# Split stores by terms, an earlier start of the first attention, and a causal mask by select, in a two-block transformer

## The chip, the cores and the metric

The kernel runs on one core of a Trainium2 chip. The metric is the device time of one execution in microseconds. In the text PE is TensorE, ACT ScalarE, DVE VectorE, POOL GpSimd and SP the sync engine, which here only issues DMAs.

## What is computed

`x` has one batch of 1024 rows of 128, the context `ctx_1024` has 6404 rows of 128. Four attentions of 16 heads of 8 follow each other, with mixtures of experts and a feed-forward layer between them (cut to what matters; layer norms, experts and residuals are left out):

```
cross0: softmax(where(mask, -inf, (x Wq) (ctx Wk)^T / sqrt(8))) (ctx Wv) Wproj     # 1024 x 6404, key padding mask
self0:  softmax((x Wq) (x Wk)^T / sqrt(8)) (x Wv) Wo                               # 1024 x 1024
self1:  the same with a causal mask: key t counts for query s only where t <= s
cross1: softmax((x Wq2) (ctx Wk2)^T / sqrt(8)) (ctx Wv2 + bv2)                     # 1024 x 6404, no mask
```

## The kernel before, in words

The order of the work is: setup of cross0, cross0, setup of self0, self0, experts, setup of self1, self1, setup of cross1, cross1, feed-forward, experts. Each engine has its own program (`block.sync`, `block.gpsimd`, `block.scalar`, `block.vector`, `block.tensor`), and these meet only at semaphores.

**Setup of an attention.** Queries and keys are projected in fp32 in jobs of 512 columns (`projection_plan`, `project`), and each job's result is split into three bf16 parts: ACT copies part 1 from PSUM (L937), DVE subtracts it for the rest (`take_rest`, L1104 is the helper `tt` that records all such subtractions), ACT copies part 2 (L942), GpSimd subtracts for part 3 (L753). For cross0 DVE first multiplies the keys with the mask (`keep`, L1176, `whole`) and makes a row of -BIG for the masked keys (L1162). SP stores the parts in DRAM (`store_parts`, L511 keys, L515 queries), four buffers in a ring (`SPLITS`). Keys are stored as three parts, queries as six terms (`Q_PARTS`), a head's 48 rows together. Cross0 has 13 key jobs and 2 query jobs; before them the context is transposed by PE (L1846) and evacuated by ACT (L917), and before that the layer norm of `x` is made and transposed by PE (`turn`). After the keys SP loads the mask row and a row of ones into every slot (`load_mask_row`, L498, L501), then stores the queries, then waits for all stores (`all_stored`).

**Staging.** A pass (one head and half of the queries in a cross attention; two heads and half of the queries in a short one) needs rows in SBUF: 48 rows of keys for each of two sides (6404 keys are cut in two halves, or there are two heads) and 48 rows of queries, in a ring of four slots. Keys come by three DMAs a side, for 3, 2 and 1 parts (`stage_keys` L529, `stage` L600), queries by one a side for each of two copies (L540, L543, L602). SP issues them in the order written: four passes ahead at first, then one a pass.

**A pass.** Pass A computes scores to find each query's maximum (`pass_a`, 28 units a pass in a cross attention, DVE reduces each, L1234 and L1193; `join_maxima`). GpSimd splits the maxima in three parts (`split_maxima`, L783, L811), PE turns them (`turn_maxima`, L1578, L1709), ACT copies them (L966, L1009), and SP puts them as three more rows behind the queries (`put_maxima`, L612, L551). Pass B computes the scores with keys on partitions less the maximum (`pass_b`), ACT makes exps into `probs` (`exps`, L1028, L986) out of a ring of three PSUM banks, and PE multiplies with the values (`values`), three steps later in a short attention, five in a cross attention. All matmuls are recorded on the helper line L1498. Maxima run ahead of pass B: 40 units before the first pass B of a cross attention, among which the 13 banks of values are projected.

**Early keys.** Cross1's keys depend on the context alone. In cross0's passes 18 to 30 one of 13 key blocks is put among the maxima (`a.items`): PE projects it, DVE copies it out (L1244), GpSimd makes all three parts (L845 to L848) and SP stores it.

**Causal mask.** In self1 pass A and pass B add -BIG where a key is ahead of the query, by a matmul of `ident_b` with `causal_a` or `causal_b` into the scores' bank, for diagonal tiles only. GpSimd's loop in a short attention is: `split_maxima(j + 1)`, then in even passes `stage_pair`, which copies values.

Of the kernel before, what the change touches and what calls it, by code (L numbers as in the profile page):

```python
# [26 lines left out]
U8 = mybir.dt.uint8  # L27
# [36 lines left out]
def projection_plan(a):  # L64

    k_jobs = [("k", "masked" if a.masked else "plain", c, min(BANK, a.keys - c)) for c in range(0, a.keys, BANK)]
    q_jobs = [("q", "plain", c * BANK, BANK) for c in range(HALVES)]
# [12 lines left out]
def short_plan(name, keys, causal):  # L80
# [7 lines left out]
    a.stage_dmas = 4 * a.sides  # L88
# [33 lines left out]
def cross_plan(name, keys, masked, early_jobs):  # L122
# [23 lines left out]
    a.stage_dmas = 4 * a.sides  # L146
# [25 lines left out]

    a.early_from, n = 16, len(a.max_units)
    early = {(a.early_from + 2 + i) * n + 4: i for i in range(early_jobs)}
    a.items, a.items_with = [], [0]
    for v in range(a.n * n):
        if v in early:
            a.items.append(("key", early[v]))
        a.items.append(("max", v))
        a.items_with.append(len(a.items))  # L180
    a.key_item = {i: k for k, (kind, i) in enumerate(a.items) if kind == "key"}
# [4 lines left out]
def transformer(nc, io, out):  # L186
    cross0 = cross_plan("cross0", 6404, masked=True, early_jobs=13)
# [10 lines left out]
    with ExitStack() as ctx:  # L198
# [17 lines left out]


# [18 lines left out]
        ROWS_IN = cross0.sides * cross0.ring * 3  # L236
# [21 lines left out]
        keep = probs_b[:, 0:S // 2].bitcast(BF16)  # L258
        mask_in = probs_b[:, S // 2:S // 2 + S // 4].bitcast(U8)
        drop_row = k_stages[0:1, 0:S]  # L260
        part_words = SPLITS * 3 * BANK // 2
        for a in attentions:


            if a.masked:
                a.whole, a.rest = scratch[:, 0:SPLITS * BANK], scratch[:, SPLITS * BANK:2 * SPLITS * BANK]
                a.parts = probs_b[:, 16 * BANK - part_words:16 * BANK]
            else:
                a.whole, a.rest = probs_b[:, 0:SPLITS * BANK], probs_b[:, SPLITS * BANK:2 * SPLITS * BANK]
                a.parts = probs_b[:, 2 * SPLITS * BANK:2 * SPLITS * BANK + part_words]  # L270
            a.whole = a.whole.rearrange("p (b n) -> p b n", b=SPLITS)
# [3 lines left out]


        early_whole, early_rest = (z[:, b * 4:(b + 1) * 4].rearrange("p t d -> p (t d)") for b in range(2))
        early_parts = xn[:].rearrange("p t d -> p (t d)")[:, 0:3 * BANK // 2].bitcast(BF16).rearrange(
            "p (t n) -> p t n", t=3)
# [51 lines left out]
        n_first = len(loads)  # L331
        weight("o_cross0", [P, D], io["L0_xattn_Wproj"])
# [1660 lines left out]
```

## Time and profile before

| | us |
|---|---|
| median of 3 runs | 2730.98 (2729.42 to 2733.01) |
| the profiled execution | 2728.58 |
| its span | 2726.7 |
| PE busy | 2384.8 (87%) |
| DVE busy | 2352.2 (86%) |
| ACT busy | 2134.0 (78%) |
| POOL busy | 274.8 (10%) |
| setup and first maxima of cross0, to the first pass B | 0 to 136 |
| cross0, passes | 136 to 1114 |
| self0, with its setup | 1114 to 1340 |
| self1, with its setup | 1394 to 1588 |
| cross1, setup | 1588 to 1631 |
| cross1 | 1631 to 2640 |

The busy shares are means over stages with different limits. In each stage the question is which wait ends last. The mean granted TensorE clock is 0.941 of full speed.

### The profile page before, as it was taken

Reading aid. Unit: us, or ns where it says so; the run is one execution under the profiler, and the core shown is the slowest. Engines: PE = TensorE matmul, PEld = TensorE weight load, DVE = VectorE, ACT = ScalarE, POOL = GpSimd, SP = SyncE. Lnnn points to the kernel's source line nnn. Section 1 sums busy time; section 2 is a strip of 40 time slices with the busy share of each in tenths; the row PEclk is TensorE's granted clock in tenths of the full one; section 3 lists DMA queues with packets and bytes.
Section 4 is the critical chain, followed back from the end, with each engine's and each line's share of the span. In section 5 each row is a group of like instructions: output and inputs, shape, how many; then the busy total and the mean of one; then the engine's idle time right before and its main releaser. Section 6 shows DMA issues by size and latency. Waiting matters only on the chain.

```text
span 2726.7 us, 59202 instructions
## 1 busy us (share of the span) xinstructions
PE 2384.8 (87%) x23163; PEld 751.8 (28%) x23163; DVE 2352.2 (86%) x2668; ACT 2134.0 (78%) x4065; POOL 274.8 (10%) x740
## 2 busy tenths in 40 slices
PE   4499999999999999489758848999999999999986
PEld 2222222222222222122322213222222222222224
DVE  6699999999999997499636649999999999999945
ACT  3189999999889899469615625999999999999971
POOL 5000110012111110100001100000000100000000
PEclk8799999999999999789878968999999999999998
DMA  4201111111111110111121030111111111111000
GB/s 144 73 24 41 41 35 45 43 44 41 47 49 41 41 43 7 46 50 33 36 61 41 30 99 4 38 34 30 30 40 33 30 30 41 31 30 32 17 3 8
DMA packets 75513, 107.98 MB, mean 40 GB/s; under 512 B 17061, under 2 KB 55849, under 8 KB 75241
## 3 DMA queue, kind: packets, MB, share of 16 engines
q1 hardware_dynamic: 73128, 99.79, 12.4%
q0 software_dynamic: 2112, 4.42, 0.9%
q8 instruction: 189, 3.10, 0.5%
q14 instruction: 84, 0.68, 0.1%
HBM read 73.45 MB, written 21.90 MB: 35 GB/s over the span
## 4 chain that ended last, share of the span: by engine, by line
PE 68%; DVE 18%; ACT 5%; SPq 3%; issue 3%; DMA 2%; POOL 0%; ACTq 0%; DVEq 0%
PE ps L1498 68%; DVE maxima L1234 12%; ACT probs L1028 4%; SPq L515 1%; DVE maxima L1193 1%; SPq L600 1%; ACT probs L986 1%; DVE scratch L1104 1%; DMA o_self<-acc_out 0%; PE ps L1504 0%; DVE stats L1110 0%; DMA scratch<-o_self 0%; DMA q_stages<-max_rows 0%; DVE z L1104 0%; DMA q_stages<-q_cross 0%
## 5 line engine op out<-in xcount | busy, mean ns | idle before, releaser
L1234 DVE TENSOR_REDUCE maxima<-ps 128x1 f32<-128x920 f32 x1792 | 1887.8, 1111 | 96.4 <-PE ps L1498 96.3
L1028 ACT ACTIVATE probs<-ps 128x512 f32<-128x512 f32 (+1 forms) x3264 | 1761.3, 594 | 159.9 <-PE ps L1498 159.7
L1498 PE MATMUL ps<-probs,v_stage 128*16 128x256 f32 x14208 | 1159.5, 393 | 0.6 <-ACT acc_out L1017 0.4
L1498 PE MATMUL ps<-k_stages,q_stages 64*128 64x460 bf16 (+2 forms) x4032 | 756.3, 373 | 187.3 <-DMA q_stages<-q_cross 64.4
L1498 PE MATMUL ps<-q_stages,k_stages 64*128 64x512 bf16 (+1 forms) x3712 | 725.8, 381 | 45.1 <-ACT probs L986 16.9
L1498 PEld LDWEIGHTS ps<-k_stages,q_stages 64*128 64x128 bf16 x4032 | 193.6, 93 | 1049.7 <-issue 494.3
L1498 PEld LDWEIGHTS ps<-probs,v_stage 128*16 128x16 f32 x14208 | 236.9, 94 | 412.2 <-issue 362.9
L1193 DVE TENSOR_REDUCE maxima<-ps 128x2 f32<-128x1024 f32 (+1 forms) x224 | 240.1, 1108 | 94.5 <-PE ps L1498 90.9
L986 ACT ACTIVATE probs<-ps 128x512 f32<-128x512 f32 x448 | 224.2, 554 | 72.7 <-PE ps L1498 71.7
L1498 PEld LDWEIGHTS ps<-q_stages,k_stages 64*128 64x128 bf16 x3712 | 187.4, 93 | 277.4 <-ACT probs L1028 69.4
L952 ACT ACTIVATE by_key<-ps 128x512 f32<-128x512 f32 (+1 forms) x30 | 17.5, 583 | 146.2 <-PE ps L1498 146.2
L759 POOL COPY v_stage<-by_key 128x400 f32<-128x400 f32 x64 | 33.1, 517 | 901.1 <-PE ps L1498 785.8
L811 POOL CAST half_parts<-neg_max 128x4 bf16<-128x4 f32 x64 | 11.9, 187 | 851.4 <-DVE neg_max L1253 794.5
L1104 DVE TENSOR_TENSOR scratch<-scratch 112x512 f32<-112x512 f32 (+1 forms) x14 | 13.6, 982 | 66.0 <-DMA scratch<-acc_out 39.7
L904 ACT ACTIVATE std<-var_eps 128x4 f32<-128x4 f32 x18 | 3.7, 205 | 70.9 <-DVE var_eps L1116 70.9
L1104 DVE TENSOR_TENSOR probs<-ps,probs 128x512 f32<-128x512 f32 x36 | 24.5, 689 | 19.8 <-ACT probs L1088 8.2
L1017 ACT ACTIVATE acc_out<-ps 128x512 f32<-128x512 f32 x64 | 38.2, 597 | 0.3 <-PE ps L1498 0.3
L1504 PE MATMUL ps<-ident,z 128*128 128x128 f32 x32 | 8.1, 403 | 32.0 <-DVE z L1126 18.5
L1504 PE MATMUL ps<-ident,xn 128*128 128x128 f32 x24 | 6.6, 430 | 31.5 <-DVE xn L1104 18.0
L783 POOL CAST max_parts<-neg_max 128x8 bf16<-128x8 f32 x32 | 6.1, 189 | 208.5 <-DVE neg_max L1204 162.4
L753 POOL TENSOR_TENSOR probs<-probs 128x512 bf16<-128x512 f32 x10 | 11.2, 1151 | 149.8 <-ACT probs L942 149.8
L1104 DVE TENSOR_TENSOR z<-ps,z 128x512 f32<-128x512 f32 (+2 forms) x10 | 6.7, 674 | 21.0 <-PE ps L1498 14.6
(233 smaller groups left out, 965.4 us busy)
## 6 DMA issues: line engine op xcount, KB each, us to landing
q_stages<-q_cross SPq DMA_DIRECT2D x256, 48.0 KB, 2.6
k_stages<-k_cross SPq DMA_DIRECT2D x64, 150.2 KB
k_stages<-k_cross SPq DMA_DIRECT2D x64, 150.0 KB
scratch<-acc_out SPq DMA_DIRECT2D x496, 16.0 KB
k_stages<-k_cross SPq DMA_DIRECT2D x64, 100.1 KB
k_stages<-k_cross SPq DMA_DIRECT2D x64, 100.0 KB
q_stages<-q_self SPq DMA_DIRECT2D x32, 192.0 KB
k_cross<-probs SPq DMA_DIRECT2D x12, 384.0 KB, 2.8
```

The costliest lines, as they stand in the source:

```text
L515: sp.dma_start(a.q_dram[:, term * E:(term + 1) * E, c0:c0 + n], src[:, part, 0:n]).then_inc(done, DMA)
L600: sp.dma_start(k_stage(a, slot)[base + row:base + row + parts_ * E, :], a.k_dram[0:parts_, h * E:(h + 1) * E, :]).then_inc(done, DMA)
L759: nc.gpsimd.tensor_copy(v_stage[:, par, 0:full, 0:E], src[:, 0:full, :]).then_inc(sem(a.name + "_v_staged"), 1)
L952: last = nc.scalar.activation(by_key[:, t:t + full, :], src[:, 0:full, :], ACT.Copy)
L986: return nc.scalar.activation(probs[:, i % a.p_slots, low:BANK], ps[:, b_bank(a, use), low:BANK], ACT.Exp, scale=float(E) ** -0.5)
L1017: nc.scalar.activation(acc_out[:], ps[:, ACC_BANK, :], ACT.Copy).then_inc(sem(a.name + "_acc_copied"), 1)
L1028: return nc.scalar.activation(probs[0:m, probs_slot(a, j, i), :], ps[0:m, b_bank(a, use), :], ACT.Exp, scale=float(E) ** -0.5)
L1104: return nc.vector.tensor_tensor(out_, a, b, op)
L1193: nc.vector.tensor_reduce(pair_maxima[:, j % 2, :, qt % QT, c // BANK], ps[:, A_BANK + 2 * (g % 2):A_BANK + 2 * (g % 2) + 2, 0:n], AX_X, A ...
L1234: nc.vector.tensor_reduce(maxima[:, at, seg:seg + 1], ps[:, A_BANK + 2 * (k % 2):A_BANK + 2 * (k % 2) + 2, 0:a.segment], AX_XY, ALU.max).t ...
L1498: return nc.tensor.matmul(out_, lhsT, rhs, start=start, stop=stop)
L1504: last = nc.tensor.transpose(ps[:, bank, t * P:(t + 1) * P], src[:, b * QT + t, :], ident[:])
```

## The change

What it does, part by part. (1) The context is transposed first and the layer norm's result later, between the split jobs (`SETUP_TURNS`). `x` is loaded behind the first piece of context. The mask is loaded in one partition only, the keys are no longer multiplied with it, and the row of -BIG alone masks them. Constants that are needed later are made later on GpSimd. The mask row and ones row are loaded by 2 + 2 DMAs. (2) Key parts are stored as six terms, like the queries, in arrays `[TERMS, P, n]`, by three DMAs a job (`store_job`); ACT issues those of the last query job, and the stores waited for are fewer. Staging takes one DMA a side for keys. In a short attention the first pair takes half of its queries first (`stage_rest` for the others). (3) The 13 early key blocks move from cross0's passes to its first maxima (`a.fill`), with ACT making the copy and parts 1 and 2, GpSimd the rest and part 3. (4) In self1's even passes SP puts the maxima before it stages. (5) Pass B's causal mask matmuls are gone; GpSimd's `affine_select` writes zeros into the exps instead (`clear`), and `values` waits for it.

```diff
+        a.fill = [("values", i, n * (i + 1) // banks - (n * (i + 1) % banks == 0)) for i in range(banks)]
+        a.fill += [("key", i, 2 * i + 1) for i in range(early_jobs)]
...
+        def store_job(queue, a, i):
+            kind, c0, n = a.jobs[i]
+            src, done = a.parts[:, i % SPLITS, :, 0:n], stored(a, i)
+            queue.wait_ge(sem("split_part3"), a.jobs_before + i + 1)
+            first = 0
+            for part, terms in enumerate((3, 2, 1)):
+                if kind == "k":
+                    dst, part_ = a.k_dram, src[:, 0:terms]
+                else:
+                    dst, part_ = a.q_dram, src[:, part:part + 1].to_broadcast([P, terms, n])
+                queue.dma_start(dst[first:first + terms, :, c0:c0 + n].rearrange("a p c -> p a c"),
+                                part_).then_inc(done, DMA)
+                first += terms
...
             def stage_keys(a, j):
-                    for row, parts_ in ((0, 3), (3 * E, 2), (5 * E, 1)):
-                        sp.dma_start(dst[base + row:base + row + parts_ * E, 0:count],
-                                     a.k_dram[0:parts_, h * E:(h + 1) * E, first:first + count]).then_inc(done, DMA)
+                    sp.dma_start(dst[base:base + ROW_MAX, 0:count],
+                                 a.k_dram[:, h * E:(h + 1) * E, first:first + count]).then_inc(done, DMA)
...
+                if a is cross0:
+                    for i in range(len(early.jobs)):
+                        if i == len(early.jobs) - 2:
+                            put_maxima(0)
+                        store_job(sp, early, i)
+                else:
+                    put_maxima(0)
...
+                    if a.turn_step[j] == 0 and j + 1 < a.n:
+                        put_maxima(j + 1)
                     if half == 0 and pair >= 1 and pair + a.ring - 1 < H // 2:
                         ...
                         stage(pair + a.ring - 1)
-                    if j + 1 < a.n:
+                    if a.turn_step[j] != 0 and j + 1 < a.n:
                         put_maxima(j + 1)
...
+                def clear(j, t):
+                    if not is_diagonal(a, j, t):
+                        return
+                    kt, low = a.steps[j][t]
+                    width = (kt % QT + 1) * P - low
+                    for side in range(a.sides):
+                        i = pair_tile(a, j, t, side)
+                        pool.wait_ge(sem(a.name + "_probs"), i + 1)
+                        tile = probs[:, i % a.p_slots, low:low + width]
+                        nc.gpsimd.affine_select(out=tile, in_=tile, compare_op=ALU.is_ge, fill=0.0, base=P - width,
+                                                pattern=[[1, width]], channel_multiplier=-1).then_inc(sem("cleared"), 1)
                 for j in range(a.n):
                     pair, half = a.passes[j]
                     if j + 1 < a.n:
                         split_maxima(j + 1)
-                    if half == 0 and 1 <= pair < H // 2 - 1:
-                        pool.wait_ge(sem(a.name + "_batches"), a.batches_before[j])
-                        stage_pair(pair + 1)
+                    for t in range(len(a.steps[j])):
+                        if t == 2 and half == 0 and 1 <= pair < H // 2 - 1:
+                            pool.wait_ge(sem(a.name + "_batches"), a.batches_before[j])
+                            stage_pair(pair + 1)
+                        clear(j, t)
...
+            def take_early(i):
+                _, _, n = early.jobs[i]
+                b = i % SPLITS
+                act.wait_ge(sem("split_psum"), early.jobs_before + i + 1)
+                if i >= SPLITS:
+                    act.wait_ge(sem("split_rest"), early.jobs_before + i - SPLITS + 1)
+                    act.wait_ge(stored(early, i - SPLITS), stored_count(early, i - SPLITS))
+                whole = early.whole[:, b, 0:n]
+                nc.scalar.activation(whole, ps[:, EARLY_BANK, 0:n], ACT.Copy).then_inc(sem("early_whole"), 1)
+                act.wait_ge(sem("early_whole"), i + 1)
+                nc.scalar.activation(early.parts[:, b, 0, 0:n], whole, ACT.Copy).then_inc(sem("split_part1"), 1)
...
         pass_b:
-                    if diag:
-                        hi = (kt % QT + 1) * P
-                        for side in range(a.sides):
-                            bank = b_bank(a, pair_tile_use(a, j, t, side))
-                            mm(ps[:, bank, low:hi], ident_b[:], causal_b[:, 2 * P - (hi - low):2 * P],
-                               start=False).then_inc(sem(a.name + "_scores"), 1)
         values:
+                    if a.causal:
+                        pe.wait_ge(sem("cleared"), diagonals_before(a, j, 2 * b + 2))
...
+            def cross0_before(i):
+                if i in SETUP_TURNS:
+                    b = SETUP_TURNS.index(i)
+                    if b == 1:
+                        half_turned(0, 1)
+                    turn(b, xn, 1, 3)
```

## Rows read from the trace of the kernel before

**Rows 1.** Chain that ended last, setup: start us, us, what

```profile
55.87 0.87 SPq L498
...
71.57 0.59 SPq L515
...
81.21 0.78 SPq L529
...
85.50 7.81 DMA q_stages<-q_cross
...
100.55 24.64 DVE maxima L1234 x24
```

**Rows 2.** Timeline, setup of cross0: start us, us, engine line op

```profile
13.37 1.13 DVE L1126 TENSOR_SCALAR xn<-x,mean_var,rstd 128x128 f32<-128x128 f32 x4
...
22.70 1.02 PE L1498 MATMUL ps<-ctxT,w_kv_cross 128*128 128x512 f32 x2
...
40.03 0.63 ACT L937 ACTIVATE probs<-scratch 128x512 bf16<-128x512 f32 x1
...
42.11 1.22 POOL L753 TENSOR_TENSOR probs<-scratch,probs 128x512 bf16<-128x512 f32 x1 [1.29 <-ACT probs L942]
...
54.34 0.69 DVE L1104 TENSOR_TENSOR scratch<-ps,probs 128x512 f32<-128x512 f32 x1 [0.64 <-ACT probs L937]
```

**Rows 3.** Key stores: the page (last: us to landing) and SP issue ns

```profile
k_cross<-probs SPq DMA_DIRECT2D x12, 384.0 KB, 2.8
...
L511 SPq DMA_DIRECT2D k_cross<-probs x13: 359/360/392, 29.3 to 55.4; - x13
```

**Rows 4.** Windows: engines busy; at the end PEclk, DMA share, GB/s

```profile
95.00:100.00 5.00, 4.77 (x22) 3.41 (x22) 3.87 (x5) 0.60 (x1) 0.00 (x0) 0.54 0.36 118
...
1590.00:1595.00 5.00, 1.43 (x12) 1.32 (x12) 4.69 (x18) 0.85 (x2) 0.00 (x0) 0.96 0.25 88
```

**Rows 5.** Timeline, first maxima of either cross attention

```profile
135.93 0.64 PE L1498 MATMUL ps<-q_stages,k_stages 64*128 64x512 bf16 x2
...
1638.91 1.17 PE L1498 MATMUL ps<-w_v_cross,ctxT 128*128 128x128 f32 x8
```

**Rows 6.** Timeline, GpSimd, one row a pass: plain, then with early keys

```profile
156.62 0.19 POOL L811 CAST half_parts<-neg_max 128x4 bf16<-128x4 f32 x1 [28.13 <-PE ps L1498]
...
186.73 0.19 POOL L811 CAST half_parts<-neg_max 128x4 bf16<-128x4 f32 x1 [13.25 <-DVE neg_max L1253]
...
700.66 0.19 POOL L811 CAST half_parts<-neg_max 128x4 bf16<-128x4 f32 x1 [13.26 <-DVE neg_max L1253]
...
731.81 0.19 POOL L811 CAST half_parts<-neg_max 128x4 bf16<-128x4 f32 x1 [13.25 <-DVE neg_max L1253]
```

**Rows 7.** Timeline, setup of self0

```profile
1138.98 4.49 POOL L753 TENSOR_TENSOR probs<-probs 128x512 bf16<-128x512 f32 x4 [22.11 <-ACT probs L942]
...
1159.26 0.61 PE L1498 MATMUL ps<-k_stages,q_stages 64*128 64x512 bf16 x2 [19.58 <-DMA q_stages<-q_self]
```

**Rows 8.** Groups by shape, self1: xcount, busy us, mean ns

```profile
L1498 PE MATMUL ps<-causal_b,ident_b 128*128 128x128 bf16 x108 | 16.2, 234 | 0.0
```

**Rows 9.** Timeline: a select at the start; self1 round a turn of maxima

```profile
2.46 0.29 POOL L696 TENSOR_SCALAR_AFFINE_SELECT ident<-ident 128x128 f32<-128x128 f32 x1 [0.24 <-POOL ident L695]
...
1457.97 0.29 PE L1498 MATMUL ps<-causal_b,ident_b 128*128 128x128 bf16 x2
...
1459.48 0.23 PE L1578 MATMUL ps<-ident_b,max_parts 128*24 128x128 bf16 x1
...
1462.83 1.53 SPq L612 DMA_DIRECT2D q_stages<-max_rows  x2
...
1466.06 0.39 PE L1498 MATMUL ps<-q_stages,k_stages 64*128 64x512 bf16 x2 [1.51 <-DMA q_stages<-max_rows]
```

**Rows 10.** Timeline, setup of cross1

```profile
1587.30 19.92 SPq L529 DMA_DIRECT2D k_stages<-k_cross  x24
...
1630.86 0.95 PE L1498 MATMUL ps<-k_stages,q_stages 64*128 64x460 bf16 x4 [22.94 <-DMA q_stages<-q_cross]
```

More of the change, by code:

```diff
@@ L235, in transformer @@
         SIDE = P // 2
-        ROWS_IN = cross0.sides * cross0.ring * 3
+        ROWS_IN = cross0.sides * 2
         QT = NT // HALVES
@@ L375, in transformer @@
             before = attentions[:attentions.index(a)]
-            a.jobs_before = sum(len(b.jobs) for b in before)
+            a.jobs_before = sum(len(b.jobs) for b in before) + (a is not cross0) * len(early.jobs)
             a.banks_before = sum(len(b.v_banks) for b in before)
-            a.k_dram = dram("k_" + a.name, [3, P, a.keys], BF16)
-            a.q_dram = dram("q_" + a.name, [H, TERMS * E, N], BF16)
-            a.staged_before = sum(b.stagings // b.ring * b.stage_dmas for b in before)
+            a.k_dram = dram("k_" + a.name, [TERMS, P, a.keys], BF16)
+            a.q_dram = dram("q_" + a.name, [TERMS, P, N], BF16)
             if not a.cross:
                 a.o_dram = dram("o_" + a.name, [4, 2, P, BANK], F32)
+        early.jobs_before, early.k_dram = len(cross0.jobs), cross1.k_dram
         def size(a, kt):
@@ L430, in pair_tile, with is_diagonal, diagonals_before @@
             return 2 * (a.steps_before[j] + t) + side
+        def is_diagonal(a, j, t):
+            return a.causal and a.steps[j][t][0] // QT == a.passes[j][1]
+        def diagonals_before(a, j, t):
+            return a.sides * sum(is_diagonal(a, i, u) for i, u in a.all_steps[:a.steps_before[j] + t])
         def pair_goal(a, j, t):
@@ L447, in moe1_banks, with q_rest_count @@
             return (5, 6, 7) if u % 2 == 0 else (0, 1, 2)
+        def q_rest_count(a):
+            return (1 + (a is self1)) * 2 * a.sides * DMA
         def b_bank(a, use):
@@ L958, in short_attention, with fill @@
+            def fill(a):
+                for kind, i in itertools.chain(*a.fill):
+                    if kind == "values":
+                        take_values(a, i)
+                    else:
+                        take_early(i)
+                if a is cross0:
+                    early_part2(len(early.jobs) - 1)
             def short_attention(a):
@@ L1774, in cross_attention @@
                         turn_maxima(0)
-                given = a.items_with[a.ahead]
+                if a is cross0:
+                    pe.wait_ge(sem("early_whole"), len(early.jobs))
+                given = a.ahead
                 for j in range(a.n):
```

438 lines of the change are left out of this document (222 added, 216 removed).

## The prediction

> **What bounds the kernel now.** I read the page first: over the whole span PE, DVE and ACT are each busy most of the time, so what counts is where all three stand still. The chain of waits for the first 100 us shows the largest such place [rows 1]: from 55.87 to 93.3 no engine computes. SP alone works, first on 24 small copies of the mask row and the ones row, from 71.57 on twelve stores of query parts, from 81.21 on staging pass 0, which lands 7.8 us after its last issue. Then the first maxima go at DVE's pace, 24.64 us for 24 units, 1.03 each. The second view is the timeline of one engine over many passes: GpSimd splits maxima once a pass, 30.11 us apart in a plain pass and 31.15 in one that carries an early key block [rows 6]. The third is the timeline of each later setup: self0's first maxima start 20 us after the first split part is begun [rows 7]; cross1's wait 22.94 us for query rows [rows 10]. The last is self1's loop, where PE is the engine with hardly a gap, except for the wait on a row of maxima behind SP's staging [rows 9].
>
> **Part 1, setup of cross0.** Layer norm still ends at 14.5 [rows 2], so the first remainder can't be taken earlier than 14.6; the context transposes no longer wait for it, and the first key block's part 1 comes at about 14.3, where it was 21.8. From there a job costs ACT three steps of about 0.6 (evacuate context, part 1, part 2), 1.85 us; DVE one subtraction from PSUM, 0.69, and a row of mask; GpSimd 1.22; SP three issues of 0.36 [rows 2, 3]. The key parts are stored by terms, six copies where there were three, so 768 KB a job. The DMA rate at full share is 88/0.25 = 352 GB/s [rows 4], so 2.2 us a job. The ring of four buffers says the same: 4.0 us from part 1 to part 3, 0.7 of issue, 2.8 to land [rows 3] and 1.1 for the added bytes are 8.6 for four jobs. I take 2.15 (bounds 1.85, and 2.5 as now). The last key job's part 1 is then at 40 to 41, its part 3 at 45, stored at 49. The mask row takes 2 issues of SP instead of 24 (the ones row's two are issued before the jobs) and lies under that wait, q0's three stores too; q1's go to ACT. Staging of pass 0 begins at 49.1 and waits once, for q0 (51.4). How long it takes is unknown: each side's keys come in one DMA in place of three. Now it is 93.3 - 81.2 = 12.1 us [rows 1]; at the full rate 800 KB would take 2.3 and land with 2.4. Window rows put me between: during cross1's staging 88 GB/s moved at a share of 0.25, so only 4 engines of 16 were at work, 22 GB/s each [rows 4], and one larger copy should spread better. I take 7.3. First maxima at 56.4 in place of 93.4: **-37.0** (-43 to -27).
>
> The Trainium skill, "DMA: Bandwidth & Descriptors", section on why a DMA increments its semaphore by 16, says that a copy is spread over the largest number up to 16 that divides the slowest dimension of both sides. By that rule today's three loads of a side use 3, 2 and 8 engines and the lowest one carries 17 of 48 rows; after the change it is 6 engines with 8 rows each. The share of 0.25 agrees; by the rule the staging would take about 6.7 us, the sum 0.6 less. It also speaks against the change: query rows would go from 16 engines to 6, which is still under a pass.
>
> **Part 2, early keys in the maxima phase.** A unit of maxima costs PE about 0.3; a value bank 1.17 [rows 5]; an early key block 1.02 [rows 2]. For the first 28 units: 28 x 0.29 + 13 x 1.17 + 13 x 1.02 = 36.6, plus 3.5 because the clock stands at 0.54 after the idle stretch [rows 4] for the first 7 us. That is 40 against 31.4 now (93.4 to 124.8): +8.6, and PE replaces DVE as the bound. ACT has 13 x (0.6 + three of 0.6) = 32, GpSimd 2 x 1.2 x 13 = 31: covered. Not covered: job 4 must wait for the store of job 0, and that stands on SP behind four passes of staging (24 issues of 0.7, to 67) and on the DMA behind their 3.2 MB (to about 75). It lands at 78, PE would be there at 74: +3.7. The twelve units after it go as now. ACT also waits for all early stores before the first exps; I have them land at 111, as pass B begins (135.93 now [rows 5]). In sum **+12.3** (+5 to +17).
>
> **Part 3, loop of cross0.** Thirteen key blocks leave the passes: 13 x (31.15 - 30.11) [rows 6] = **-13.6**. The later constants on GpSimd (some 17 us) lie between two splits of maxima that are 30 us apart. SP's six issues a pass replace ten.
>
> **Part 4, setup of self0 and self1.** Part 3 of the four jobs ends 1.12 us apart from 1140.1 [rows 7]. Three of them are stored by SP in nine issues of 0.36, bound by 2.3 MB at 352 GB/s, landed at about 1149 (now 1151.6); then four loads of half the queries instead of eight issues, 2.8, and 3.2 to land: 1155.1 for 1159.3. The same in self1: **-8.4** for both (-5 to -10). The rest of the queries has eight units of maxima to arrive (four in self1).
>
> **Part 5, loop of self1.** Maxima are put ahead of the staging in even passes: SP now begins at 1462.83 after eight issues, PE waits until 1466.06 [rows 9]. The wait shown is 1.51; four pairs stage, so 4 x 1.6 = **-6.5**. The mask matmuls: a pair of 128 wide holds PE for 0.22 us, 64 pairs (108 single rows and 16 wide ones are in the trace [rows 8]), 15.6 us in all. In the odd passes PE is the bound; in the even ones ACT takes over for two steps. I count 70%: **-11** (-6 to -16). In their place 128 selects on GpSimd, 0.29 each [rows 9], two in a step of 1.2 to 1.5 us; the values come three steps later, so nobody waits. But GpSimd works in order: the split of the next maxima now stands behind the last select of an odd pass. Exps of that tile end about 0.3 us after 1458.2 shifted, two selects to 1458.9, four linked steps of 0.27 to 1460.1; PE wants the turn 1.08 us after 1457.97, at 1459.05 (with both mask pairs gone; now it is 1459.48 [rows 9]). Seven times 1.0: **+7** (0 to +9).
>
> **Part 6, setup of cross1.** Now 24 key loads keep SP until 1607.2 and the DMA beyond, so that q stores issued from 1610.33 land at 1628.5 and maxima start at 1630.86 [rows 10]. After: eight loads, issued by 1593; with 22 GB/s an engine their 2.4 MB are through by 1607 if six engines share them, by 1616 if it stays at 88 GB/s. Then q0 with three issues lands at 1614, two loads of 0.7 and 2.3: 1617.9. **-13** (-5 to -14).
>
> **The sum.** -37.0 + 12.3 - 13.6 - 8.4 - 6.5 - 11 + 7 - 13 = -70.2. The profiled run took 2728.58 with a span of 2726.7; it lies 2.4 under the median of 2730.98. So 2658.4 for such a run and 2660.8 as a median.
>
> **The rivals.**
> - *The memory side binds twice.* Stores by terms double what keys write. If a setup job takes 2.9 us in place of 2.15 (+9) and an early job 3.6 in place of 2.8 of PE's time (+10), the time is 2680. For: ACT waited for key stores twice already; against: the share in the store stretches is near a half. 0.14.
> - *All goes well.* No stall at job 4, mask matmuls count in full, no late turn: -3.7 - 4.6 - 7 give 2645. 0.12.
> - *The early keys hold nothing free:* a pass stays at 31.15, since something other than the key item made it long: 2674. The period changes exactly where the keys begin, so 0.02.
> - *Slower.* Term-major loads run on one DMA engine. A pass then needs (600 + 192) KB / 22 GB/s = 36 us on it, over the 30.1 of a pass; it decides from there on, two engines (18 us) would not. 56 passes x 6 us is +336, near 3000. A store of the same pattern lands in 2.8 us [rows 3], a load of it isn't in the trace. 0.02.
>
> **How the numbers follow.** The forecast has 0.70, with its own range 2648 to 2674. The range reaches over the first two rivals and to what a bound of part 1 adds to each: 2645 - 6 is 2639, and 2680 + 6 is 2686. About 0.2% is what a measurement of this kernel can tell from no change; only the last rival is beyond it on the slow side: faster 0.97, same 0.01, slower 0.02.
>
> **What would show it.** First maxima at 56 and pass B at 111; PE without gaps in the 28 units but one, on ACT's key copy; GpSimd's splits 30.1 apart in all of cross0; a PE wait of about 1 us for the split maxima in self1's even passes and none for rows of maxima; cross1's first maxima 17 to 18 us after the first layer-norm transpose there instead of 30.6. It is wrong if the staging still takes 12 us, or if PE waits for selects.

## The result and the profile after

The changed kernel takes 2702.66 us (median of four runs, 2701.78 to 2702.69) beside 2731.74 for the kernel before (2729.42 to 2733.01): a ratio of 0.9894, interval 0.9877 to 0.9911, so 29 us less. The forecast was 2660.8 with a range of 2639 to 2686: right in sign, wrong in size, by 42 us. The profiled execution has a span of 2700.1 us, 26.6 under that of before. The page of after, which is to be held against the small table of the profile before:

```profile
span 2700.1 us, 58859 instructions
...
PE 2368.9 (88%) x23035; PEld 742.6 (28%) x23035; DVE 2333.7 (86%) x2629; ACT 2154.6 (80%) x4104; POOL 294.5 (11%) x848
...
PEclk7799999999999999799768868999999999999998
```

Such a page says almost nothing of where 42 us went; the boundaries of the stages do. In the timeline each attention has three marks: its first matmul of pass A (k_stages,q_stages), its first of pass B (q_stages,k_stages) and the end of its last. The differences of the marks, in us:

```
stretch                          before    after   change  forecast
start to first A of cross0        93.45    66.12   -27.3    -37.0   part 1
first A to first B of cross0      42.48    57.38   +14.9    +12.3   part 2
first B to end of cross0         977.25   965.70   -11.6    -13.6   part 3
end of cross0 to first A, self0   46.08    42.43    -3.7     -4.2   part 4
first A to end of self0          177.36   176.16    -1.2      0
end of self0 to first A, self1    85.92    82.84    -3.1     -4.2   part 4
first A to end of self1          164.51   180.72   +16.2    -10.5   part 5
end of self1 to first A, cross1   43.81    30.36   -13.5    -13     part 6
first A of cross1 to span's end 1095.84  1098.39    +2.6      0
```

One row has nearly two thirds of the miss: the causal attention was to lose 10.5 us and gained 16.2. The setup of cross0 has another 9.7. Each column of marks is of one profiled execution. In three kernels of this case that have the same causal attention (this one and two of the runs below) its stretch takes 180.7, 181.7 and 183.6 us, so that a difference of some 3 us between two profiles is no finding by itself.

**Inside the causal attention.** Timeline of the kernel after round one even pass, L653 puts maxima, L625 and L633 stage keys and queries, L665 stores the previous pass's output, L1082 is ScalarE's eviction into the buffer that L665 empties, L1660 the turn of the split maxima:

```profile
1429.28 1.49 SPq L653 DMA_DIRECT2D q_stages<-max_rows  x2
1430.81 0.78 SPq L625 DMA_DIRECT2D k_stages<-k_self  x1
...
1433.91 1.43 SPq L633 DMA_DIRECT2D q_stages<-q_self  x2
1435.38 2.60 SPq L665 DMA_DIRECT2D o_self<-acc_out  x4
...
1441.10 0.60 ACT L1082 ACTIVATE acc_out<-ps 128x512 f32<-128x512 f32 x1 [5.11 <-DMA o_self<-acc_out]
...
1451.19 0.23 PE L1660 MATMUL ps<-ident_b,max_parts 128*24 128x128 bf16 x1 [0.85 <-POOL max_parts L856]
```

The maxima do go out first now, at 1429.28. But the output of the pass before, evicted from 1431.16 to 1431.76, is behind six staging issues: its four stores are issued from 1435.38 to 1437.98, and the next eviction waits 5.11 us, to 1441.10, until they have landed. Before, the staging stood ahead of both, maxima and store, in this order, and TensorE's wait for the maxima was the only one to be seen [rows 9]. There, too, the store was behind the staging's issues, eight then; but the staging didn't wait for the maxima, so it was over (1462.79) before the output was evicted. SyncE and ScalarE of the kernel before:

```profile
1458.29 1.87 SPq L600 DMA_DIRECT2D k_stages<-k_self  x3
1462.29 0.60 ACT L976 ACTIVATE acc_out<-ps 128x512 f32<-128x512 f32 x1
1464.40 2.50 SPq L624 DMA_DIRECT2D o_self<-acc_out  x4
```

From the end of the eviction to the first issue of its store it took 1.5 us there (1462.89 to 1464.40) and takes 3.6 now (1431.76 to 1435.38). The groups by line of ScalarE over the causal attention have the sum (busy us, mean ns, then idle before and its releasers). Before:

```profile
L976 ACT ACTIVATE acc_out<-ps 128x512 f32<-128x512 f32 x16 | 9.6, 601 | 1.7 <-PE ps L1498 1.1 <-DMA o_self<-acc_out 0.7
```

and after:

```profile
L1082 ACT ACTIVATE acc_out<-ps 128x512 f32<-128x512 f32 x16 | 9.6, 601 | 23.2 <-DMA o_self<-acc_out 22.0 <-PE ps L1581 1.3
```

0.7 us of waiting for the store have become 22.0: four waits of 4.9 to 6.2 us, one behind each of the four stagings, and two of 0.4. TensorE gets this as waits for the exponentials, which ScalarE makes behind its evictions. The group of pass B's score matmuls over the same stretch, before and after:

```profile
L1498 PE MATMUL ps<-q_stages,k_stages 64*128 64x512 bf16 (+1 forms) x192 | 35.3, 364 | 18.0 <-DMA q_stages<-max_rows 8.9 <-ACT probs L986 8.7
L1581 PE MATMUL ps<-q_stages,k_stages 64*128 64x512 bf16 (+1 forms) x192 | 36.8, 380 | 38.4 <-ACT probs L1092 28.8 <-DMA q_stages<-max_rows 5.4 <-POOL v_stage L842 3.8
```

**In the setup.** The chain of waits of after, where [rows 1] and [rows 2] have that of before:

```profile
22.24 4.19 DMA k_cross<-probs
26.47 0.04 issue
26.52 0.60 ACT probs L1010
27.11 0.53 ACT probs L1015
...
27.71 1.16 POOL probs L823
28.89 0.36 SPq L504
...
29.82 4.46 DMA k_cross<-probs
...
37.72 4.23 DMA k_cross<-probs
...
45.34 5.22 DMA k_cross<-probs
...
53.95 4.48 DMA q_cross<-probs
...
59.18 6.80 DMA q_stages<-q_cross
```

The chain goes round the four buffers, three jobs a turn, 7.6 to 7.9 us: more than half of it a key store on its way, 4.2 to 5.2 us where it was 2.8 [rows 3]. The windows of after say why (engines busy; at the end PEclk, DMA share, GB/s):

```profile
20.00:50.00 30.00, 16.48 (x50) 6.89 (x48) 17.83 (x21) 15.11 (x30) 12.66 (x12) 0.83 1.01 310
50.00:66.00 16.00, 0.00 (x0) 0.00 (x0) 0.69 (x1) 1.75 (x3) 2.26 (x2) 0.50 0.64 195
```

The DMA share (the busy share of the 16 DMA engines) is 1.01 from 20 to 50 us, at 310 GB/s: they are busy for the whole of it, and no engine of the core is busy for more than 60% of it. The 24 row copies of [rows 1] are gone and cost two issues, as forecast.

### The profile page after: what moved, and what is told of

Same layout as the page of the kernel before. It is cut to its first block, busy times and chain, and to the rows that moved or that the text cites. A ratio compares the mean times of both kernels' runs of the same rounds, so it can differ in the third digit from the quotient of the medians.

```text
span 2700.1 us, 58859 instructions
## 1 busy us (share of the span) xinstructions
PE 2368.9 (88%) x23035; PEld 742.6 (28%) x23035; DVE 2333.7 (86%) x2629; ACT 2154.6 (80%) x4104; POOL 294.5 (11%) x848
## 4 chain that ended last, share of the span: by engine, by line
PE 69%; DVE 15%; ACT 5%; DMA 4%; SPq 3%; issue 3%; POOL 1%; ACTq 0%; DVEq 0%; POOLq 0%
PE ps L1581 68%; DVE maxima L1333 11%; ACT probs L1135 3%; DMA k_cross<-probs 1%; DMA o_self<-acc_out 1%; SPq L504 1%; DVE maxima L1292 1%; SPq L633 1%; ACT probs L1092 1%; SPq L665 1%; POOL probs L823 1%; DVE stats L1224 0%; SPq L625 0%; PE ps L1587 0%; DMA scratch<-o_self 0%
## 5 line engine op out<-in xcount | busy, mean ns | idle before, releaser
L1581 PE MATMUL ps<-k_stages,q_stages 64*128 64x460 bf16 (+2 forms) x4032 | 753.5, 372 | 144.4 <-DVE maxima L1333 57.4
L1581 PE MATMUL ps<-q_stages,k_stages 64*128 64x512 bf16 (+1 forms) x3712 | 728.4, 382 | 68.8 <-ACT probs L1092 36.9
L896 POOL CAST half_parts<-neg_max 128x4 bf16<-128x4 f32 x64 | 11.9, 186 | 835.7 <-DVE neg_max L1343 804.9
L1218 DVE TENSOR_TENSOR scratch<-scratch 112x512 f32<-112x512 f32 (+1 forms) x14 | 13.6, 981 | 66.3 <-DMA scratch<-acc_out 39.7
L873 POOL TENSOR_SCALAR_AFFINE_SELECT probs<-probs 128x128 f32<-128x128 f32 (+1 forms) x128 | 38.4, 309 | 111.2 <-ACT probs L1092 108.4
L1082 ACT ACTIVATE acc_out<-ps 128x512 f32<-128x512 f32 x32 | 19.2, 599 | 24.4 <-DMA o_self<-acc_out 22.0
L1124 ACT ACTIVATE acc_out<-ps 128x512 f32<-128x512 f32 x64 | 38.2, 597 | 0.3 <-PE ps L1581 0.3
L1010 ACT ACTIVATE probs<-ps 128x512 bf16<-128x512 f32 (+1 forms) x25 | 14.7, 589 | 27.7 <-PE ps L1581 14.7
L1048 ACT ACTIVATE probs<-ps 128x512 f32<-128x512 f32 (+1 forms) x13 | 7.6, 581 | 30.2 <-PE ps L1581 20.9
```

The lines of the kernel that those rows point to most:

```text
L873: nc.gpsimd.affine_select(out=tile, in_=tile, compare_op=ALU.is_ge, fill=0.0, base=P - width, pattern=[[1, width]], channel_multiplier=-1) ...
L1124: nc.scalar.activation(acc_out[:], ps[:, ACC_BANK, :], ACT.Copy).then_inc(sem(a.name + "_acc_copied"), 1)
L1218: return nc.vector.tensor_tensor(out_, a, b, op)
L1581: return nc.tensor.matmul(out_, lhsT, rhs, start=start, stop=stop)
```

## The experiments

Theory 1: SyncE's staging between the maxima and the store of the output is what the causal attention pays for. Theory 2: it is the selects on GpSimd. For the setup, theory A: the doubled key stores fill the DMA engines; rival B: the ring of buffers and its order.

**Order undone.**

```
+ (behind the staging, in every pass)
  if j + 1 < a.n: put_maxima(j + 1)
- (ahead of the staging, in even passes)
```

> The changed kernel with one part undone: in the causal self-attention SyncE issues the maxima behind the staging of the next pass again, as before. Theory 1 (the six staging transfers that now stand between the maxima and the store of the previous pass's output keep ScalarE's eviction waiting for that store, 22.0 us in six waits): these waits go, ScalarE's waits for the maxima come back (forecast at 6.5 us in the sum), so the attention's stretch from its first pass A to its last matmul falls from 180.7 to about 165 to 168 us, and the median from 2702.7 to 2687 to 2690. Theory 2 (the selects on GpSimd and the turns that wait for them cost it, and the order is worth its 6.5 us): the stretch grows to about 187 us and the median to 2709.

Measured: 2687.8 us (2686.2 to 2691.2), ratio to before 0.9842, interval 0.9826 to 0.9859; the stretch of the causal attention 163.8 us, a little under theory 1's 165. Theory 2 is out.

**Selects undone.**

```
- nc.gpsimd.affine_select(out=tile, in_=tile, ..., fill=0.0, ...)
+ mm(ps[:, bank, low:hi], ident_b[:], causal_b[:, 2 * P - (hi - low):2 * P], start=False)
```

> The changed kernel with the other part undone: the causal mask is added by TensorE's matmuls again and GpSimd's selects are gone, the new order of the maxima stays. Theory 1 (order): the waits for the store of the output stay, about 20 us in six, and the median is 2700 to 2707. Theory 2 (selects): the late turns go, the stretch falls from 180.7 to about 165 us, and the median to 2687.

Measured: 2713.5 us (2709.4 to 2714.3), ratio 0.9930 [0.9913, 0.9947]; the stretch 187.8 us. Slower than the changed kernel by 11: above theory 1's 2707, and far from theory 2's 2687. I had counted the selects at nothing here; they are worth 7.1 us of the stretch even with the wrong order. In the evictions' group 22.9 us are waited for the store.

**Both undone.**

> The changed kernel with both parts undone, so that only the setups, the early keys and the key copies are new. Both theories: the stretch of the causal attention comes back to the 164.5 us of before, and the median is 2702.7 - 16.2 = 2686.5, from 2684 to 2690. Should it stay above 2695, the stretch is long because of the new setup or the new key copies in memory, and neither the order nor the selects.

Measured: 2693.5 us (2690.9 to 2696.9), ratio 0.9866 [0.9849, 0.9882]; the stretch 167.4 us. That is 3.5 us above the upper end of the range that I gave and under the 2695 from which the setup or the key copies were to be blamed. The stretch stays 2.9 us above the 164.5 of before, which is about what two profiles of the same code can differ by.

**The store ahead of the staging.**

```
  if a.turn_step[j] == 0 and j + 1 < a.n:
      put_maxima(j + 1)
+     if 1 <= j < a.n - 1:
+         store_out(j - 1)
  ... stage(pair + a.ring - 1)
```

> The changed kernel with one move: in the even passes of the causal self-attention SyncE issues the maxima first, then the store of the previous pass's output, and the staging last. Theory 1: both waits are gone, for the maxima and for the store; the stretch falls from 180.7 to 158 to 162 us and the median to 2680 to 2684. Theory 2 (selects): nothing moves, 2700 to 2703.

Measured: 2680.8 us (2677.0 to 2682.8), ratio 0.9818 [0.9801, 0.9834]; the stretch 156.7 us. This is the run that settles it: one move of issues on SyncE, nothing else, and 21.9 us of median; the stretch is even a little under the 158 to 162 expected. SyncE in its timeline, and the eviction's group:

```profile
1431.22 1.48 SPq L653 DMA_DIRECT2D q_stages<-max_rows  x2
1433.73 2.50 SPq L665 DMA_DIRECT2D o_self<-acc_out  x4
1436.28 0.77 SPq L625 DMA_DIRECT2D k_stages<-k_self  x1
```

```profile
L1084 ACT ACTIVATE acc_out<-ps 128x512 f32<-128x512 f32 x16 | 9.6, 600 | 3.4 <-DMA o_self<-acc_out 2.1 <-PE ps L1583 1.3
```

The wait fell from 22.0 to 2.1 us, and TensorE's waits for the exponentials in the group above from 28.8 to 9.1. The four combinations of order and mask can now be read off as a square: with the old order the selects take 3.6 us from the stretch (167.4 to 163.8), with the new one 7.1 (187.8 to 180.7); the new order adds 20.4 with matmuls and 16.9 with selects. The medians give the same picture: the selects take 5.7 and 10.8 us, the order adds 20.0 and 14.9. Of the selects' part the smaller value, 3.6, is within what two profiles differ by; the median of 5.7 is the better one.

**Keys in DRAM as three parts again.**

```
- dst, part_ = a.k_dram, src[:, 0:terms]        (three stores, 3 + 2 + 1 terms)
+ queue.dma_start(a.k_dram[:, :, c0:c0 + n].rearrange("a p c -> p a c"), src)
+ for row, parts_ in ((0, 3), (3 * E, 2), (5 * E, 1)):   (staging: three loads a side)
```

> The changed kernel with the keys in DRAM as three parts again: each key job is stored by one transfer of 384 KB instead of three of 768 KB together, and each side of a pass is staged by three transfers instead of one; all the rest is as in the changed kernel. Theory A (the first setup is bound by the doubled key stores: the 16 DMA engines are busy with a share of 1.01 at 310 GB/s from 20 to 50 us): the share in that stretch falls under 0.7, the first pass A starts at 60 to 63 us instead of 66 to 70, less the 1 to 2 us that four more staging issues a side cost SyncE, and the median falls by 2 to 6 us, unless the loops' twelve staging issues a pass give it back. Rival B (the ring of the splits on ScalarE and VectorE bounds the setup, and bytes don't matter): the stretch before the first pass A is within 1.5 us of 68, and the median rises by 2 to 4 us for the issues.

Measured: 2742.4 us (2737.9 to 2743.4), ratio 1.0042 [1.0033, 1.0052]. The median is far out of what I expected, and yet the setup did what theory A says. Windows of this kernel:

```profile
20.00:50.00 30.00, 13.00 (x48) 6.10 (x46) 16.83 (x22) 16.03 (x32) 14.52 (x13) 0.82 0.64 215
```

The share is 0.64 instead of 1.01, and the first pass A starts at 60.6 us. In the profiles of the changed kernel, of the four runs above and of the one with late staging below, whose setups are the same, it starts between 66.1 and 70.1 (mean of the six 68.3), so the halved stores are worth 7.7 us, four more staging issues already taken off. What costs more than this gains are the loads, three a side: the maxima phase of cross0 takes 68.8 us (57.4), self0 from its first pass A on 185.3 (176.2), the causal attention 197.0 (180.7), the setup of cross1 44.9 (30.4). In the causal attention ten issues instead of six are now ahead of the store of the output, and the eviction's wait grows with them:

```profile
L1085 ACT ACTIVATE acc_out<-ps 128x512 f32<-128x512 f32 x16 | 9.6, 600 | 33.8 <-DMA o_self<-acc_out 32.5 <-PE ps L1584 1.3
```

and in the setup of cross1 the picture of [rows 10] is back: 24 key loads in front of the query stores, the last of which then lands after 16 us. The chain of waits there:

```profile
1622.73 0.48 SPq L505
...
1623.26 16.03 DMA q_cross<-probs
...
1640.13 2.60 DMA q_stages<-q_cross
```

**ScalarE's second part first.**

```
+ part 2 of job i - 1   (its block moved up, unchanged)
  part 1 of job i       (waits for the store of job i - 4)
- part 2 of job i - 1
```

> The changed kernel with one move: on ScalarE the second part of a job is written before the first part of the next job instead of behind it, so that it doesn't stand behind that job's wait for the stores. Theory A (the stores' bytes bound the setup): the first pass A starts where it did, 66 to 70 us, and the median stays within 3 us of 2702.7. Rival B (the ring bounds it: the second part waits behind a store that isn't its own): 3 us or more earlier, the median 2698 or less.

Measured: 2701.65 us (2700.2 to 2703.3), ratio 0.9893 [0.9873, 0.9913], first pass A at 65.97. For the first setup no difference can be measured (the lowest of the six profiles above is 66.1): with the stores at a share of 1, the order on ScalarE doesn't matter there. Theory A. The setup of cross1, whose splits have the same order, took 28.5 us, under the 29.5 to 31.8 of the profiles with the old order; it is one profile, and the median moved by 1.0 us only.

**Passes 2 and 3 staged late.**

```
- for j in range(a.ring):            stage_keys(a, j); stage_queries(j)
+ for j in range(2):                 ...
  early stores, put_maxima(0)
+ for j in range(2, a.ring):         stage_keys(a, j); stage_queries(j)
```

> The changed kernel with one move on SyncE: passes 2 and 3 of the first cross-attention are staged behind the early key stores and the maxima of pass 0, not ahead of them. Theory (the staging of 1.2 MB in front of the first early store holds the ring of the early jobs: that store landed after 9.5 us, and TensorE had half of its time idle from 80 to 90 us with its clock down): from the first pass A to the first pass B it takes 49 to 52 us instead of 57 to 58.6, and the median falls by 6 to 8 us. Rival (the early jobs cost by themselves, by the work of ScalarE and GpSimd in that phase): it takes 56 to 58.6 us, and the median moves by less than 2 us.

In the changed kernel the chain of waits has this stall, right behind SyncE's staging of passes 1 to 3:

```profile
77.28 9.47 DMA k_cross<-probs
86.86 0.61 ACT probs L1048
87.50 6.93 PE ps L1581 x16
```

With the staging moved a store in this place lands faster:

```profile
83.12 4.02 DMA k_cross<-probs
87.16 0.04 ACTq L1049
87.20 0.04 issue
87.25 0.61 ACT probs L1051
```

Measured: from first A to first B 52.8 us instead of 57.4 (49 to 52 expected), but the median is 2700.6 (2699.2 to 2705.7), ratio 0.9885 [0.9866, 0.9905]: 2 us, not 6 to 8. The phase is shorter than its rival allowed, 56 or more; in the whole nothing is shown by this run, as the intervals of the two kernels overlap. The profiled execution is the slowest of the four (2705.7), with a late first A (69.1) and 183.6 us in the causal attention.

**Staging rows over more DMA engines.**

```
- a.k_dram[:, h * E:(h + 1) * E, first:first + count]
+ a.k_dram[:, h * E:(h + 1) * E, first:first + count].rearrange("a e c -> e a c")   (keys and queries)
```

> The changed kernel with the staging transfers' rows in another order, keys and queries alike: the slowest dimension of the source is the head's 8 columns instead of the 6 terms. The Trainium skill's page on DMA bandwidth and descriptors (the section on why a DMA counts by 16) has a transfer spread over as many engines as divide the slowest dimension of both sides, so over 8 instead of 6. If that is so, the last staging transfers ahead of the first pass A land 1 to 1.5 us earlier, each of the four attentions starts earlier by about 1 us, and the median falls by 2 to 5 us; if the number of engines is not set so, or the transfers share the engines anyway, it stays within 2 us of 2702.7.

Measured: 2694.1 us (2690.4 to 2695.5), ratio 0.9862 [0.9841, 0.9883], 8.6 under the changed kernel: more than expected. The four setups hardly moved (first A at 67.6; 42.0, 82.3 and 30.1 us for the other three, from 42.4, 82.8 and 30.4); the gain is in the maxima phase of cross0, 54.7 us for 57.4, in cross1 behind its first A, 1096.3 for 1098.4, and most of all in the causal attention, 174.5 for 180.7, where the eviction waits 18.1 us for the stores instead of 22.0: loads that are done sooner are out of the way of the store behind them. How many engines a load uses can be read where key loads alone are under way, in the setup of cross1. Windows of the changed kernel, then of this one:

```profile
1578.00:1584.00 6.00, 0.00 (x0) 0.00 (x0) 5.62 (x27) 0.41 (x2) 0.00 (x0) 0.50 0.38 152
1571.00:1577.00 6.00, 0.00 (x0) 0.00 (x0) 5.62 (x28) 0.41 (x2) 0.00 (x0) 0.50 0.51 161
```

The DMA share is 0.38 and then 0.51: six engines of 16, and then eight. That agrees with the Trainium skill's rule ("DMA: Bandwidth & Descriptors", section "Why a DMA increments its semaphore by 16 and not by 1"). The rate rose by 6% and not by a third, though, so eight engines moved less each than six did, and what the time gained is not in proportion to the engines.

**Three moves together.** (The last two and the store's.)

> Three of the earlier edits together on the changed kernel: the store of the previous output ahead of the staging in the causal attention (21.9 us by itself), the staging rows in the order that spreads over 8 engines (8.6), and passes 2 and 3 staged behind the early stores (2.1). If they act on different waits they add up to 32.6 us and the median is 2670; the causal attention's part of the 8 engines (6.2 us of its stretch) lies in the same waits that the store's move takes away, so that 2674 to 2677 is likelier. From 2672 to 2679 they are taken to overlap there; at 2680 or more, the move of the store was all.

Measured: 2669.8 us (2668.3 to 2672.2), ratio 0.9775 [0.9762, 0.9789]. In the median they add up in full, 32.8 us; the overlap that I took for likelier isn't seen there. In the causal attention it is: its stretch is 154.1 us, 2.6 under the 156.7 of the store's move alone, where the rows over more engines had taken 6.2 by themselves. Which stretch makes up for it, these profiles of one execution each can't tell.

**The same, and cross0's keys alone as three parts.** (Its key loads and query loads are in the old row order again.)

> The same three edits, and the first cross-attention's keys alone in DRAM as three parts, so that its setup stores 384 KB a job instead of 768 KB; its staging takes three transfers a side. From the first of these kernels with three parts (first pass A at 60.6 us instead of 66 to 70) the setup gains 7 us; its maxima phase loses what four more staging issues a side cost, of which two passes now stand behind the early stores: 2 to 5 us; and the loop's staging has a whole pass of 30 us to be early in, nothing. So the median is 2 to 5 us under that of the three edits alone. If the long maxima phase there (68.8 us) came from the twelve issues a pass and not from the two passes staged ahead, it is above it.

Measured: 2662.45 us (2661.4 to 2663.8), ratio 0.9747 [0.9734, 0.9760]: 7.4 less, more than the 2 to 5 expected. First A at 59.4, first B at 110.4, the stretch between them 50.9 us. So the long phase with three parts (68.8) came from passes 2 and 3 staged ahead of the early stores, and the loads' issues hide once those are out of the way.

**Both undone, with the rows over more engines.**

> The changed kernel with order and selects undone and the staging rows in the order of 8 engines. The causal attention took 167.4 us with both undone and 164.5 us in the kernel before, where the loads of its maxima phase were spread over other counts of engines. Theory (the slower landing of 6-engine staging is that difference): the stretch is 163 to 165.5 us and the median 6 to 9 us under the 2693.5 of both undone. Rival (it is something else): the stretch stays at 167 to 168.

Measured: 2681.7 us (2678.5 to 2685.4), ratio 0.9816 [0.9801, 0.9831]; the stretch of the causal attention 162.5 us for 167.4. Both moved by more than the theory said (11.8 us of median for 6 to 9, and a stretch under its 163 to 165.5). So the staging's landing counts in this stretch; that it is what the 2.9 us over the kernel before were, isn't shown, since the stretch is now 2.0 under that. In the group of the matmuls of pass B the wait for rows of maxima, which stand behind the staging there, is 7.9 us where it was 9.7 in the same window, less than half of the 4.9.

**The second part first, once more.**

> The last kernel (three moves, the first cross-attention's keys as three parts) with ScalarE's second part of a job ahead of the first part of the next, as in the run that changed only this. Theory (with 384 KB a job the transfers no longer bind the setup, their share is 0.61 from 20 to 50 us, and the chain of waits goes round the ring: the wait for the store of four jobs ago, then part 1, part 2 of the job before, part 3, the store, 5.2 to 7.6 us for three jobs): with the second part out of that wait the ring goes over four jobs, and the first pass A starts 2 to 5 us earlier than 59.4 us; the median is 2658 to 2661. Where the stores bound it, the same move was worth 1.0 us in the median. Rival (TensorE's transposes of the context and their evictions set the setup's pace now): the first pass A starts within 1 us of 59.4, the median within 1.5 us of 2662.5.

Measured: 2658.98 us (2657.8 to 2661.4), ratio 0.9737 [0.9724, 0.9751], the fastest of all. The first A moved by only 0.4 us, to 58.98: on that mark the rival is right, and the theory's 2 to 5 us fall. Its picture is half right. The chain of waits has no key store in it any more:

```profile
28.60 0.70 DVE scratch L1236
29.35 0.51 issue
29.86 0.59 ACT probs L1034
30.47 0.70 DVE scratch L1236
...
41.76 3.13 DMA q_cross<-probs
...
50.00 8.85 DMA q_stages<-q_cross
```

A job takes 1.87 us (28.60 to 30.47) in a chain of ScalarE and VectorE, but q0's stores start only 1.1 us earlier than they did (41.76 for 42.90), and 8.85 us of staging stand behind them all the same. In the profiles the setup of cross1, whose splits have the same order, is shorter (29.1 us; 31.5 in the kernel this one is compared with, 30.2 in the one of three moves). The median is where the theory had it, 3.5 us lower, but the intervals of the two ratios overlap, and where those us would come from is not settled.

## Why the prediction was wrong, by its own steps

**Part 5, order of SyncE in the causal attention: -6.5 forecast; this step failed.** It priced the wait that the move removes and not the one that it makes. SyncE is one queue with three customers in an even pass: maxima, staging, store of the output. The step asked who waits for the maxima and put them first; it didn't ask what the staging, which now itself starts only when the maxima are there, would then hold up. Measured +16.9 with everything else equal, and -7.1 once the store was moved along with the maxima (163.8 to 156.7). TensorE's waits for rows of maxima say the same: 11.9 us with the old order, 5.4 with the new one. So the 6.5 were there to be had, though the sign that no such wait would be left didn't come; the kernel as changed paid 22.0 us of eviction waits instead. The row was in reach: the store's free semaphore is on ScalarE's path once a pass, and a pass lasts 10 us, with 4.5 of staging, 2.6 of issue and 3.1 of landing in it (in the kernel after: 1430.81 to 1435.38, to 1437.98, to 1441.10).

**Part 5, mask and late turn: -11 and +7, net -4; right within the noise.** Measured, where the order doesn't disturb, -3.6 in the stretch and -5.7 in the median. The turn's wait is in the groups by line of TensorE over the causal attention, after:

```profile
L1660 PE MATMUL ps<-ident_b,max_parts 128*24 128x128 bf16 x16 | 3.9, 243 | 6.7 <-POOL max_parts L856 6.1
```

6.1 us, forecast 7. Beside it 3.8 us of TensorE's waits are put down to GpSimd's copies of values, which stand among its selects; the prediction didn't have them. With the store moved the whole stretch comes to 156.7 us, 7.8 under before, for a forecast of 10.5; the 153.9 us of the kernel with cross0's keys as three parts, 10.6 under before, have the rows over more engines in them, which the forecast didn't.

**Part 1: -37.0 forecast, -27.3 in the profile, -25.1 by the mean of the six profiles.** The mechanism was right, the term of a job mis-sized: 2.15 us forecast, some 2.55 measured (7.6 to 7.9 for three). By the measured rate it comes out: 768 KB at 310 GB/s are 2.5 us. I had allowed 1.1 us for the added bytes in the store's landing; it grew by 1.4 to 2.4 at a share of 1, and the rate there was 310 GB/s and not 352. My own upper bound of 2.5 was the value. 7.7 us of the miss come back with 384 KB a job. The staging, 7.3 forecast, took about 10.9 (first issue 55.26, first A 66.12): 3.2 of them until q0 had landed, 2.3 forecast, and 7.7 behind that, 5.0 forecast. q1's stores from ScalarE's queue were under way beside it; that they are the reason wasn't tried. The 6.7 us worked out from the Trainium skill's rule ("DMA: Bandwidth & Descriptors", the same section) fall with the 7.3: both took the loads to be alone. Two readings were loose. The share of 0.25 was said to agree with that rule for the old loads; if the lowest engine carries 17 of 48 rows, the share is 48/17/16 = 0.18 while it works without a pause. The rule is borne out by the 0.38 and 0.51 above instead. And where no engine was said to compute, from 55.87 to 93.3, the last splits still ran at first (ScalarE 1.75 us, VectorE 0.69, GpSimd 2.26); this changes nothing in the sum.

**Part 2: +12.3 forecast, +14.9 measured.** Job 4's wait for the store of job 0 was foreseen with 3.7 us and took 5.2 of TensorE's time; it is the one large gap of TensorE in that phase, as forecast. The early stores' end came later than pass B: ScalarE turns to the exponentials at 124.7, 1.2 us after pass B's first matmul, and had waited 8.2 us for the last early store.

**Parts 3 and 4: -13.6 and -8.4 forecast, -11.6 and -6.7 measured.** The passes of cross0 are 30.11 to 30.33 us apart (the last 29.2, as before), as [rows 6] said of a plain pass, so the early blocks are out of them. Each later setup gained some half to one us less.

**Part 6: -13 forecast, -13.5 measured; right, and for the reason given.** Timeline of SyncE in the kernel after, beside [rows 10]:

```profile
1571.41 6.02 SPq L555 DMA_DIRECT2D k_stages<-k_cross  x8
1593.56 1.59 SPq L504 DMA_DIRECT2D q_cross<-probs  x3
1598.25 1.48 SPq L570 DMA_DIRECT2D q_stages<-q_cross  x2
```

With 24 loads again the run with three parts gave 14.5 of it back. Of the 2.6 us that cross1 got longer 2.1 lie in one interval, between its first two passes, 32.4 us for 30.35 before; what makes it was not tried.

**The rivals.** "The memory side binds twice" named the right resource for the setup and gave it 9 us, and the setup was longer by 9.7, some 6 of them in the jobs and the rest in the staging; its other half, 10 us in the early jobs, didn't come (2.6). It was the rival closest in kind, and it would still have been 23 us too low, since neither it nor any other looked at the queue behind the moved step. The slower rival, loads on one DMA engine, is excluded.

## What to carry to other kernels

When a step is moved forward in an in-order queue, list everything in that queue that it is moved past and everything that now stands behind the block it left, and look for each one's customer; the step that was second in line before may be the one with no slack. A step that waits for a semaphore makes all that stands behind it wait as well: the staging was in time before because it didn't stand behind the wait for the maxima. Price the wait that is created at the full length of the block (here 4.5 us of issues, which became a wait of 4.9 to 6.2 us four times), not only the one removed. And storing data twice to make its loads simpler is a trade between two phases: here it paid 13 to 14 us where loads stood ahead of something (the setup of cross1) and cost 7.7 where stores were the bound (the setup of cross0), so that leaving the first cross-attention with three parts and the others with six beat six everywhere by 7.4 us.

## What was not expected of the hardware

The DMA engines at a share of 1.01 moved 310 GB/s with 128, 256 and 384 KB stores from SBUF to DRAM, not the 352 worked out from a stretch at a share of 0.25, and a store's landing grew from 2.8 us to 4.2 to 5.2 us. Nor is 310 the rate at a full share: in the other profiles with the same stores it was 280 to 289, and the stores of cross1's query parts, with no engine computing beside them, had 339 in this window of the changed kernel:

```profile
1595.00:1598.00 3.00, 0.00 (x0) 0.00 (x0) 0.00 (x0) 0.00 (x0) 0.00 (x0) 0.50 1.01 339
```

What sets it is open.

The granted clock of TensorE in the causal attention, a mean of its two levels, went with the engine's waits: 0.88 before, 0.82 after, 0.84 with the order undone, 0.87 with the store moved ahead; pass B's score matmuls (512 columns and fewer) took 364, 380, 383 and 363 ns in the mean. A removed wait can thus be worth more than its length: of the 24.0 us that the store's move takes from the stretch (180.7 to 156.7), 5.0 are TensorE's own busy time (131.25 to 126.20), with the same 1172 matmuls in the records. The profiles of all four kernels with the store moved have 0.87 and 125.7 to 126.6 us of busy time, the five with selects that have it behind the staging 0.80 to 0.84 and 128.3 to 133.5. It isn't so in each case: with the order undone 16.9 us of waits went and the busy time stayed at 131.1. By the same coin the 20.1 us of mask matmuls that are gone from TensorE lowered its busy time by only 10.1 (141.36 to 131.25) in the changed kernel.
